# A fused gather-project, Hadamard and ternary FFN kernel: the conditioning weights in five slots instead of eight, another order at the head, and the written-out orders of the engines laid anew

## The reference, cut to what matters

```python
w = weights[conditions]                         # 64 of 200 matrices, each 64 x 64
y = einsum('bct,bcd->bdt', x, w)                # x is 64 x 64 x 512
def hbitlinear(x, w, bits):
    xq = act_quant(fwht(x), bits)               # Hadamard transform of the last axis, then 8 bit per token
    wq = weight_quant(w)                        # ternary, scale = mean |w|
    return einsum('bsd,fd->bsf', xq, wq)
h = hbitlinear(y, w_up, 8)                      # 512 -> 1024
h = square(relu(h))
out = x + hbitlinear(h, w_down, 8)              # 1024 -> 512
```

## Time and profile before

| | us |
|---|---|
| median of 3 runs | 270.84 |
| the 3 runs | 270.58, 270.84, 272.72 |
| the profiled execution, its own time | 272.7 |
| its span, first to last instruction | 270.9 |
| PE busy in it | 252.4 |
| DVE busy | 204.6 |
| ACT busy | 146.8 |
| POOL busy | 124.0 |

### The profile page before, as it was taken

One profiled execution on the slowest core, in us unless ns is written; L12 is line 12 of the kernel. 1 busy time (PEld: TensorE's weight loads), 2 busy tenths in 40 slices (PEclk: granted clock), 3 DMA queues, 4 the chain that ended last, 5 costly groups with the idle time before them and its releaser, 6 DMA issues.

```text
span 270.9 us, 6291 instructions
## 1 busy us (share of the span) xinstructions
PE 252.4 (93%) x2188; PEld 209.2 (77%) x2188; DVE 204.6 (76%) x344; ACT 146.8 (54%) x210; POOL 124.0 (46%) x135
## 2 busy tenths in 40 slices
PE   8769989999999399999999999998999999998993
PEld 8668879998897288778987888986888887775761
DVE  0157969989797555968697987896797978879872
ACT  2137898964656326375745555755556647641330
POOL 1000034657739317174657455565218174856810
PEclk9979999999999869999999999999999999999999
DMA  6666935434378183364739537748294363647433
GB/s 185 208 236 216 263 93 131 121 59 92 89 64 192 49 200 83 36 167 108 160 89 141 105 97 180 103 86 180 43 197 77 75 159 72 159 117 88 146 82 119
DMA packets 63442, 34.31 MB, mean 127 GB/s; under 512 B 53554, under 2 KB 53682, under 8 KB 63410
## 3 DMA queue, kind: packets, MB, share of 16 engines
q10 hardware_dynamic: 48370, 12.95, 29.5%
q1 hardware_dynamic: 15040, 20.95, 25.6%
HBM read 13.70 MB, written 8.39 MB: 82 GB/s over the span
## 4 chain that ended last, share of the span: by engine, by line
PE 51%; SPq 26%; issue 9%; DVE 5%; DMA 3%; ACT 2%; ACTq 1%; DVEq 0%
PE u_ps L930 14%; PE o_ps L962 13%; PE h_ps L907 12%; SPq L208 12%; SPq L206 11%; PE y_ps L866 5%; PE z_ps L882 5%; ACT uq L566 2%; DMA xs<-in_x_dram 2%; SPq L201 2%; ACTq L559 1%; DVE g L1232 1%; PE z_ps L962 1%; DVE g L1237 1%; DVE out_sb L1262 1%
## 5 line engine op out<-in xcount | busy, mean ns | idle before, releaser
L373 POOL TENSOR_TENSOR p<-g 128x512 f32<-128x512 f32 x64 | 79.3, 1269 | 25.4 <-DVE g L1237 25.3
L930 PE MATMUL u_ps<-had_sb,p 128*128 128x128 f32 x480 | 60.9, 281 | 4.3 <-ACT uq L566 4.3
L907 PE MATMUL h_ps<-zqT,w_upT 128*128 128x256 f16 x512 | 64.5, 275 | 0.5 <-DMA zqT<-zq 0.4
L930 PEld LDWEIGHTS u_ps<-had_sb,p 128*128 128x128 f32 x480 | 58.0, 196 | 7.1 <-ACT uq L566 5.6
L526 ACT ACTIVATE g<-h_ps 128x512 f32<-128x512 f32 x64 | 37.5, 596 | 39.7 <-PE h_ps L907 32.8
L962 PE MATMUL o_ps<-w_downT,uqT 128*128 128x512 f16 x240 | 56.7, 379 | 0.9 <-DVE out_sb L1262 0.9
L907 PEld LDWEIGHTS h_ps<-zqT,w_upT 128*128 128x128 f16 x512 | 50.0, 99 | 9.6 <-issue 0.8
L379 POOL TENSOR_SCALAR u_deq<-kappa,down_scale,u_abs 128x1 f32<-128x1 f32 x32 | 30.0, 939 | 52.1 <-DVE u_abs L1250 46.2
L1244 DVE TENSOR_REDUCE u_max<-u_ps 128x1 f32<-128x1024 f32 x30 | 36.7, 1222 | 20.3 <-PE u_ps L930 20.1
L566 ACT ACTIVATE uq<-u_ps,u_mul 128x1024 f16<-128x1024 f32 x30 | 33.3, 1108 | 19.4 <-DVE u_mul L1255 19.2
L962 PEld LDWEIGHTS o_ps<-w_downT,uqT 128*128 128x128 f16 x240 | 23.2, 98 | 23.2 <-DVE out_sb L1262 1.4
(11 more groups left out here) (52 smaller groups left out, 148.0 us busy)
## 6 DMA issues: line engine op xcount, KB each, us to landing
xs<-in_x_dram SPq DMA_DIRECT2D x16, 512.0 KB, 4.4
out_dram<-out_sb SPq DMA_DIRECT2D x32, 256.0 KB, 2.8
w_raw<-in_L_ffn_w_down_dram SPq DMA_DIRECT2D x4, 512.0 KB, 5.2
w_raw<-in_L_ffn_w_up_dram ACTq DMA_DIRECT2D x2, 512.0 KB, 6.5
w_raw<-in_L_ffn_w_up_dram SPq DMA_DIRECT2D x2, 512.0 KB, 4.2
ws<-in_L_cond_weights_dram SPq DMA_DIRECT2D x62, 16.0 KB, 2.4
uqT<-uq ACTq DMA_TRANSPOSE x30, 3.2
zqT<-zq ACTq DMA_TRANSPOSE x15, 3.6
```

The source lines that it names most:

```text
L373: nc.gpsimd.tensor_tensor(new[:, :, m, :], old[:, :, 0, :], old[:, :, 1, :], (ALU.add, ALU.subtract)[m]).then_inc(s_p8[k], 1)
L907: mm = nc.tensor.matmul(h_ps[:, u % 2, i, :].rearrange("p (k n) -> p k n", k=KP), w_upT[:, q, f * P:(f + 1) * P], zqT[t % NZT][:, :, q, :] ...
L930: mm = nc.tensor.matmul(home[:, c * P:(c + 1) * P], p8[t % 2][:, c, k * P:(k + 1) * P], had_sb[:, :], start=True, stop=True)
```

## The change

The slots of the gathered matrices (NW) go from eight to five. In SP's list, the w_up pieces 2 and 3 move ahead of x of tile 1, the w_down pieces forward, and several loads and stores change place. In ACT's list w_up pieces 0 and 1 go behind both of tile 0's gathers, and had_sb behind them. The lists of ACT, PE, DVE and POOL are written in another order; the calls in them are the same, each once. From the diff, cut to what is spoken of below (`negate_w` moved in it as follows: before, 12, 13 and 14 stood together ahead of quant_u(2, 1), and 15 behind relu(5, 1)):

```diff
-NX, NW, NZT, NO = 8, 8, 5, 2
+NX, NW, NZT, NO = 8, 5, 5, 2
...
 SP
             load_x(0)
             gather(0, 0)
             gather(0, 1)
+            load_up(2)
+            load_up(3)
             load_x(1)
             gather(1, 0)
             gather(1, 1)
             gather(1, 2)
             gather(1, 3)
-            load_up(2)
-            load_up(3)
+            load_down(0)
             gather(2, 0)
+            load_down(1)
+            load_down(2)
             gather(2, 1)
+            load_down(3)
...
             gather(9, 2)
+            store(0, 0)
             gather(9, 3)
...
             gather(11, 2)
-            store(0, 0)
+            load_x(8)
+            store(0, 1)
             gather(11, 3)
...
             gather(12, 2)
-            load_x(8)
-            store(0, 1)
             gather(12, 3)
+            store(1, 0)
             gather(13, 0)
             gather(13, 1)
             gather(13, 2)
+            load_x(9)
+            store(1, 1)
             gather(13, 3)
+            store(2, 0)
+            load_x(10)
+            store(2, 1)
             gather(14, 0)
             gather(14, 1)
             gather(14, 2)
             gather(14, 3)
-            store(1, 0)
+            store(3, 0)
+            load_x(11)
+            store(3, 1)
             gather(15, 0)
...
 ACT
             load_cond()
-            load_had()
-            load_up_too(0)
             load_table()
             gather_too(0, 2)
             gather_too(0, 3)
+            load_up_too(0)
             load_up_too(1)
+            load_had()
             negate_w(0)
+            y_split(0)
             weight_abs(0, 1)
-            y_split(0)
+            weight_abs(0, 3)
+            quant_z(0, 0)
             negate_w(1)
...
             square(4, 1)
-            turn_u(2, 0)
+            quant_u(2, 1)
+            y_split(8)
+            turn_u(2, 1)
             negate_w(12)
+            relu(5, 0)
...
+            quant_u(3, 1)
             negate_w(13)
-            negate_w(14)
-            quant_u(2, 1)
...
             square(6, 1)
-            relu(7, 1)
+            negate_w(14)
+            relu(7, 0)
...
             turn_u(5, 1)
-            square(8, 0)
+            negate_w(15)
+            y_split(11)
             quant_u(6, 0)
...
 PE
             project(0)
             had_z(0, 0)
-            project(1)
             had_z(0, 1)
             weight_sum(0)
             first_turn(0)
-            had_z(1, 0)
-            project(2)
+            project(1)
             weight_turn(0, 1)
             weight_turn(0, 0)
+            first_turn(1)
+            had_z(1, 0)
+            weight_turn(0, 3)
+            up(0, 0)
+            up(0, 1)
+            weight_sum(1)
+            project(2)
             had_z(1, 1)
...
             down(7, 0)
-            had_z(13, 0)
+            up(11, 2)
+            up(11, 3)
+            had_u(9, 1)
+            up(12, 1)
+            had_z(13, 1)
             project(14)
-            up(11, 2)
-            had_u(9, 1)
-            up(11, 3)
             down(7, 1)
```

More of the change, by code:

```diff
@@ L587, in _ @@
             quant_z(0, 1)
+            weight_abs(1, 1)
             weight_round(0, 3)
             weight_round(0, 2)
+            weight_abs(1, 3)
+            negate_w(2)
+            relu(0, 0)
+            relu(0, 1)
+            quant_z(1, 0)
+            square(0, 0)
+            weight_round(1, 1)
             y_split(2)
-            weight_abs(1, 1)
+            negate_w(3)
+            weight_round(1, 0)
+            relu(0, 3)
             quant_z(1, 1)
-            negate_w(3)
-            relu(0, 1)
+            relu(0, 2)
@@ L595, in _ @@
             turn_z(1)
-            relu(0, 0)
-            weight_abs(1, 3)
+            square(0, 1)
+            quant_z(2, 0)
+            weight_round(1, 3)
             y_split(3)
[L599 to L604, removed]
-            quant_z(2, 1)
[L606 to L610, removed]
@@ L611, in _ @@
-            relu(1, 0)
+            weight_round(1, 2)
+            relu(1, 1)
+            negate_w(4)
+            relu(1, 0)
+            square(1, 0)
+            relu(1, 3)
+            negate_w(5)
+            y_split(4)
+            quant_z(2, 1)
+            relu(1, 2)
             turn_z(2)
+            square(1, 1)
+            negate_w(6)
+            quant_u(0, 0)
             quant_z(3, 0)
[L614 to L617, removed]
@@ L618, in _ @@
-            square(1, 1)
-            negate_w(5)
-            negate_w(6)
+            turn_u(0, 0)
+            relu(2, 0)
+            relu(2, 1)
+            y_split(5)
+            square(2, 0)
             negate_w(7)
-            relu(2, 1)
+            relu(2, 2)
+            relu(2, 3)
             quant_z(3, 1)
-            relu(2, 0)
-            quant_u(0, 0)
+            quant_u(0, 1)
             turn_z(3)
-            square(2, 0)
-            relu(2, 3)
-            turn_u(0, 0)
+            square(2, 1)
@@ L630, in _ @@
             quant_z(4, 0)
[L631 to L634, removed]
+            turn_u(0, 1)
+            y_split(6)
             negate_w(8)
-            turn_u(0, 1)
+            negate_w(9)
             relu(3, 1)
+            quant_u(1, 0)
+            relu(3, 0)
             quant_z(4, 1)
-            relu(3, 0)
+            square(3, 0)
+            relu(3, 3)
+            relu(3, 2)
             turn_z(4)
-            y_split(6)
@@ L642, in _ @@
[L642 to L646, removed]
+            square(3, 1)
+            quant_z(5, 0)
             turn_u(1, 0)
-            quant_z(5, 0)
-            square(3, 1)
+            quant_u(1, 1)
+            y_split(7)
+            turn_u(1, 1)
+            relu(4, 0)
             negate_w(10)
             negate_w(11)
-            quant_u(1, 1)
             relu(4, 1)
-            relu(4, 0)
-            turn_u(1, 1)
@@ L670, in _ @@
[L670 to L685, removed]
+            relu(5, 0)
+            relu(5, 1)
+            square(5, 0)
+            quant_z(6, 1)
@@ L686, in _ @@
+            quant_u(3, 0)
+            relu(5, 2)
+            relu(5, 3)
+            turn_z(6)
+            square(5, 1)
+            quant_z(7, 0)
+            turn_u(3, 0)
+            quant_u(3, 1)
+            negate_w(13)
             turn_u(3, 1)
+            y_split(9)
             quant_z(7, 1)
-            y_split(9)
             turn_z(7)
             relu(6, 0)
+            relu(6, 1)
             square(6, 0)
@@ L807, in _ @@
             quant_u(12, 1)
+            turn_u(12, 1)
+            relu(15, 0)
             relu(15, 1)
[L809 to L810 removed]
             square(15, 0)
+            relu(15, 2)
+            quant_u(13, 0)
             relu(15, 3)
[L813 to L814 removed]
             turn_u(13, 0)
@@ L999, in _ @@
-            had_z(3, 1)
-            had_u(0, 0)
+            up(1, 3)
+            weight_turn(1, 2)
+            project(4)
+            up(1, 2)
+            had_u(0, 0)
+            had_z(3, 0)
+            project(5)
             up(2, 1)
             up(2, 0)
-            project(5)
-            had_z(4, 0)
-            up(2, 3)
-            up(2, 2)
-            had_u(0, 1)
-            up(3, 1)
-            had_z(4, 1)
-            up(3, 0)
-            down(0, 0)
+            had_z(3, 1)
```

531 lines of the change are left out of this document (254 added, 277 removed).

## The result

The changed kernel takes 264.27 us, median of 4 runs (263.4 to 265.09), against 271.72 for the kernel before (4 runs, 270.58 to 272.72): ratio 0.9727, 95% interval 0.9665 to 0.9788, 7.4 us less. The profiled execution took 264.8 us, its span is 263.0 against 270.9. The forecast was 262, range 258 to 268.

What follows compares the result with a forecast made beforehand. PE, busy 93% of the 270.9 us span, was taken as the bound. Gains 7.9 + 2.0 + 1.0 less 2.0 give 8.9 us: profiled 272.7 to 263.8, median 1.9 lower, 261.9, said as 262; range 258 to 268.

Steps and rivals of the forecast that it cites:

- The stall and its price: PE from 83.49 to 99.29 us: negate_w(12) to (14) queued ahead of quant_u(2, 1); moving them gains 7.9 us.
- Five slots cost 0: SP's gathers wait for project(t - 5), not project(t - 8); cost taken as 0, upper bound 7.9 us.
- The narrow places I had named: negate_w(14) and negate_w(15) in ACT's list, where gathers would land with some 2.5 us of slack.
- Gathers 9 to 11: First half, SP issuing without pause: they land one or two us ahead of their negate_w; ACT waiting costs PE little.
- rival 2: The stall moves to a late negate_w(14) or (15), PE idles and its clock falls: 270 us, no change; chance 0.07.
- Head, 2.0: Start of the kernel: earlier had_z(0, 0) and first up(0) gain 2.0 us, bounds 0 and 3.5.
- rival 3: had_sb lands last, at 16.6 us, so had_z(0, 0) gains nothing and the head's 2 us are lost: 264; chance 0.10.
- x of tile 14, 1.0: PE's wait before project(14) for its load of x disappears under more PE work: gain 1.0 us.
- Allowance for new waits, 2.0: Small waits elsewhere in the new lists cost 2 us, bounds 0 and 4.
- Rival 1 (DVE): DVE becomes next in line and half the gain returns as waits for quant scales: 266 us; chance 0.15.
- Rival 5: Slower: SP's gathers hold the loads of x, so project(9) and later ones stall: 278 us; chance 0.05.
- The signs I had named: What the later profile should show: ACT's and PE's idle and busy times, clock, start times, and SP's waits from tile 11 or 12.

Runs made afterwards that it cites:

- e1: The kernel before with only negate_w(12) to (15) moved down in ACT's list, everything else old; 262.99 us, ratio 0.9712.
- g1: The changed kernel with eight slots and negate_w(12) and (13) put back ahead of quant_u(2, 1); 271.17 us, ratio 0.996.
- e2: The changed kernel with eight slots (NW) instead of five; 262.24 us, ratio 0.9673.
- f2: The changed kernel with up(12, 1) moved behind project(14) and down(7, 1) in PE's list, relu(12, 1) behind y_split(14) in ACT's; 263.52 us, ratio 0.9681.
- g2: e4 with had_sb issued right behind the index on ACT's queue instead of last; 264.07 us, ratio 0.9702.
- f4: e1 with the first DMAs in the new order, compute lists otherwise old; 264.85 us, ratio 0.9733.
- f3: The changed kernel with gather(11, 3) ahead of load_x(8), up(12, 1) behind down(7, 1), and eight slots; 262.68 us, ratio 0.9642.
- g4: e4 with had_sb issued early and 8 constant matmuls behind project(0); 262.57 us, ratio 0.9654.
- e4: The changed kernel with gather(11, 3) moved ahead of load_x(8) and store(0, 1) in SP's list; 261.61 us, ratio 0.9657.
- g3: e4 with 12 constant matmuls added behind project(0); 264.42 us, ratio 0.9729.
- f1: The changed kernel once more, unchanged, beside the f series on one chip; 263.79 us, ratio 0.9708.

## Why the prediction was right, and where not

*The stall and its price* (7.9 us): right. e1 gives 7.9 us less (262.99 against 270.89), g1 loses them again. The reading that PE stood for a quant_u queued behind a negate_w for a far tile holds.

*Five slots cost 0*: no trace shows a cost; by the times it is open within 2 us (e2). The narrow places I had named, negate_w(14) and (15), held. (From project(10) to up(8, 0) the rows give 7.9 us, not 8.1.)

*Gathers 9 to 11*: here the step failed. I wrote that they land one or two us ahead of their negate_w and that "ACT waiting there would cost PE little, since only a relu is behind them". Two errors: I gave the last gather the median landing of 2.4 us though load_x(8) and a store stood right ahead of it in SP's queue (6.2 in the changed kernel's trace), and a relu is not little: up(4, 3) waits for it. The first could have been read from the trace before: its gather at 79.34, the first behind load_x(8) and store(0, 1), took 5.9 us to land. Measured 2.6 us in two executions of the changed kernel, nothing in f2's. Of the prediction's steps this is the one that failed in its mechanism; it is rival 2 in a milder form, at a tile where I had not put it.

*Head, 2.0*: right in size. Of the executions with the new head, leaving out those with another order of its loads or matmuls, the first had_u comes at 42.8, 43.5, 43.6, 43.8, 44.7, 45.2 and 45.4 us, median 43.8; the two with the old one (before, e1) at 47.8 and 46.5. With 1.8 us of work outstanding that is 47.1 - 43.8 - 1.8 = 1.5 us. The profiled pair's 3.2 was in part luck with the clock. Each of the two groups spreads too, by 2.6 and 1.3 us. That the first had_u comes earlier is shown; that the head's lists save time at the end is not, as e1 without them is as fast as the changed kernel. The walk gave 13.7 for had_z(0, 0) and 23.6 for the first up; measured 14.14 and 23.68. What was wrong in it: warm-up ended at 8.9, not 9.56, and had_sb came at 14.1, so that rival 3 was half true (1.2 us behind y_outer). Between 4 and 14 us the DMA engines moved 282 GB/s, between the 219 of the rival and the 300 that I had taken. In g2, where this wait for had_sb is gone, the gain didn't come out at the end.

*x of tile 14, 1.0*: the wait is gone, but it may not be the new list's doing: e1, with PE's old list, doesn't have it (its load landed after 4.2 us, not 5.4), f4 with that list has it (0.84). Beside it 1.7 us was lost before up(12, 1), whose transpose was late. I had checked project(13) and not the up that had moved ahead of project(14), whose transpose leaves with x(14).

*Allowance for new waits, 2.0*: measured 2.6 + 1.7 = 4.3, just outside my bounds of 0 to 4. In this execution 1.2 us more from the head made up for half of it. The sum came out at 7.9 us for the profiled pair, not 8.9, so two misses cancelled in part, and that is luck. The forecast of 262 was 2.3 us low: 1.0 is the sum, and the rest is the step from the profiled execution to the median, for which I took off 1.9 us; the changed kernel's profiled execution lies only 0.5 above its median.

*Rival 1 (DVE)*: fell, in e1's trace PE is busy throughout 80 to 100 us, with DVE at 16.48 of 20. *Rival 5*: no load of x was late in the changed kernel's trace; PE never waited for line 201. (Its sum adds two stalls, 15.8 us, where its words name two and the old one.)

*The signs I had named*: right were had_z(0, 0) at 14.14 and the first up at 23.68. Wrong were ACT's idle time before line 502 (4.97 us, I had said under 1.5), PE's busy time in 80 to 100 (18.26, I had said over 19), project(0) (8.88, earlier than said) and PE's last matmuls (257.72 in place of 264.82, 7.1 us earlier and not 9 to 11). SP waits for a project from tile 13 on, not 11 or 12.

Of the whole, 7.9 us of an e1 that keeps everything else against 7.4 for the full change: as it was made, the new lists, the head and the slots bring together nothing that can be measured. By the traces, the head's 1.5 and x(14)'s 1 go to two new waits. The best kernels of the study (f3 0.9642, g4 0.9654, e4 0.9657) are equal within their intervals; e4 is the changed kernel with one line moved, and takes 3.2 to 3.7% less than the kernel before. It also beats e1, which ran beside it on the same chip: its four executions (261.16 to 262.43 us) all lie under e1's (262.49 to 263.43), and the intervals of the ratios do not meet (up to 0.9679, from 0.9686). So once the gather is in its place, the rest of the change is worth 1.4 us over the four moved calls.

## What to carry to other kernels

When an engine with an in-order list stands still, look not only at what it waits for but at what is queued behind the wait: here an early negation for a tile some 90 us away held the quantization that PE needed next, and moving four calls gave as much as the whole change. Cost a DMA by what stands ahead of it in its queue, not by the median landing. And after a gain in one stage (had_sb earlier, a wait moved) look at once for the stage that gives it back.

## What was not expected of the hardware

The DMA transpose of tile 12, issued within 0.1 us of the 512 KB load of x(14), took 5.8 to 8.9 us to land in the eleven traces with the new lists (under 7.5 in two of them, g3 and g4, where PE did not wait for it), against 3.0 to 3.2 for the ones before and after it in the changed kernel. A 16 KB gather took 1.8 to 3.2 us (median 2.2) as the last one ahead of load_x(8), and 3.1 to 6.2 (median 5.6) as the first one behind it and the store, in the same eleven traces. The kernel before showed both already: its transpose at 195.29, issued 0.3 us after a load of x, took 8.6 us, and its gather at 79.34 took 5.9. No experiment here moved the transpose and the load apart, so that the load is what delays it is argued from where the slow ones lie, and not shown.

PE's clock in the head differs from execution to execution of nearly the same instructions. Stretch 12 to 24 us of the changed kernel and of f1, the same kernel; the third number from the end is the granted clock:

```profile
12.00:24.00 12.00, 7.66 (x93) 7.05 (x94) 9.37 (x21) 9.57 (x15) 0.00 (x0) 1.00 0.82 290
```

```profile
12.00:24.00 12.00, 8.66 (x74) 7.96 (x74) 7.98 (x19) 7.76 (x13) 0.00 (x0) 0.72 0.86 294
```

In the one PE never falls to its 1.2 GHz level, in the other it does for some six us, from 14 to 20 us, after the same wait for had_sb (3.20 and 2.87 us); the first up differs by 1.8 us, and the two executions by 1.5 us (264.8 and 266.27). A gain of one us in this head can't be read from one trace.
